# Graph attention on one Trainium2 core: the rows' product with the edge lengths, on VectorE for the next group or on ScalarE for the group two ahead

## What is computed

```python
edge_features = concatenate([h[dst], h[src] * dir_w, dir_w, lower_adj_feat])
edge_attr = edge_features @ W_ee + b_ee
for i in range(3):                      # 3 heads of 128 features
    q, k, v = (x @ Wq[i] + bq[i]), (x @ Wk[i] + bk[i]), (x @ Wv[i] + bv[i])
    e = edge_attr @ We[i] + be[i]
    alpha = (q[dst] * (k[src] + e)).sum(-1) / sqrt(128)
    w = softmax of alpha over the edges of each dst
    out = segment_sum((v[src] + e) * w, dst).mean over heads + x @ Ws[i] + bs[i]
    x = relu(out + residual)
```

## Time and profile before

| | us |
|---|---|
| median of 3 runs | 4367.55 |
| lowest and highest | 4361.53, 4377.33 |
| the profiled execution | 4329.4 |
| its span | 4327.6 |

### The profile page before, as it was taken

How to read it: one execution, slowest core, us unless ns; L and a number is a source line. 1 busy time by engine, 2 the same in 40 slices (tenths; PEclk the granted TensorE clock), 3 DMA queues, 4 the chain that set the end, 5 groups by cost and what they waited for, 6 DMA issues and landing times. The chain is left out here.

```text
span 4327.6 us, 82914 instructions
## 1 busy us (share of the span) xinstructions
PE 3495.6 (81%) x22381; PEld 2067.5 (48%) x22381; DVE 1823.4 (42%) x5369; ACT 1433.0 (33%) x3483; POOL 1862.8 (43%) x1907
## 2 busy tenths in 40 slices
PE   4999999947758888876777777667777769999998
PEld 2666666635534444443444444334443444555564
DVE  4666666647523333332333333323333323344222
ACT  3555555522623333332233323222222223122112
POOL 2555555500256665653566656456666630000000
PEclk8999999979879999998888998878898889999999
DMA  5677775656444554555666666556666645443223
GB/s 139 187 200 199 198 196 167 165 115 204 140 136 137 140 136 131 139 137 136 169 176 172 176 175 179 156 155 167 167 164 168 166 111 176 171 177 118 74 97 125
DMA packets 716528, 675.29 MB, mean 156 GB/s; under 512 B 382359, under 2 KB 542945, under 8 KB 716117
## 3 DMA queue, kind: packets, MB, share of 16 engines
q1 hardware_dynamic: 622598, 466.26, 37.1%
q0 software_dynamic: 77008, 200.24, 17.2%
q10 hardware_dynamic: 16768, 6.91, 0.6%
HBM read 530.84 MB, written 142.28 MB: 156 GB/s over the span
## 5 line engine op out<-in xcount | busy, mean ns | idle before, releaser
L2293 POOL DMA_INDIRECT l_y<-s_lrows,l_src x1344 | 1352.6, 1006 | 964.3 <-issue 352.4
L2373 PE MATMUL ps<-l_y,aw_pT 128*63 128x277 f32 x2700 | 436.8, 467 | 259.9 <-ACT aw_pT L2591 249.1
L3404 PE MATMUL ps<-nl_adj,nl_table 126*128 126x504 bf16 (+1 forms) x3150 | 631.4, 357 | 2.3 <-DVE nl_table L3639 2.3
L998 POOL DMA_INDIRECT em_gs<-s_rows,em_idx x400 | 432.3, 1081 | 325.8 <-DVE em_a L1189 147.9
L2357 PE MATMUL ps<-aw_yT,aw_qt 128*63 128x384 f32 x1800 | 377.2, 529 | 120.0 <-DMA aw_yT<-s_dxT 61.2
L3404 PEld LDWEIGHTS ps<-nl_adj,nl_table 126*128 126x128 bf16 x3150 | 301.8, 96 | 299.0 <-issue 5.3
L2750 DVE COPY aw_axd<-ps 128x252 f32<-128x252 f32 x225 | 94.7, 421 | 796.9 <-remote 409.9
L2330 PE MATMUL ps<-ident,l_y 128*128 128x128 f32 x1800 | 281.5, 292 | 150.9 <-issue 83.1
L2373 PEld LDWEIGHTS ps<-l_y,aw_pT 128*63 128x63 f32 x2700 | 195.7, 154 | 431.9 <-ACT aw_pT L2591 279.6
L2591 ACT ACTIVATE aw_pT<-ps 128x381 f32<-128x381 f32 x225 | 109.9, 488 | 736.8 <-remote 506.0
L2577 ACT ACTIVATE aw_yT<-ps 128x512 f32<-128x512 f32 (+1 forms) x525 | 261.4, 536 | 245.2 <-remote 114.7
(11 more groups left out here) (381 smaller groups left out, 5866.1 us busy)
## 6 DMA issues: line engine op xcount, KB each, us to landing
nl_adj<-s_adj SPq DMA_DIRECT2D x20, 3100.8 KB
aw_yT<-s_dxT SPq DMA_DIRECT2D x150, 384.0 KB
aw_geoS<-s_geoS SPq DMA_DIRECT2D x450, 94.5 KB
nl_adj<-s_adj SPq DMA_DIRECT2D x15, 2325.6 KB
ws_msg<-s_msg SPq DMA_DIRECT2D x75, 384.0 KB, 3.8
s_dxT<-aw_yT SPq DMA_DIRECT2D x75, 384.0 KB
aw_qt<-s_qt SPq DMA_DIRECT2D x225, 126.0 KB
s_msg<-em_msg SPq DMA_DIRECT2D x100, 256.0 KB
```

What stands on the lines that cost most here:

```text
L998: pool.indirect_dma_start(out=gs[:, u, j, :], out_offset=None, in_=d["rows0"], in_offset=bass.IndirectOffsetOnAxis(ap=slot[:, u, 2 * j:2 * ...
L2293: pool.indirect_dma_start(out=y[:, u, j, 0:W], out_offset=None, in_=table, in_offset=bass.IndirectOffsetOnAxis(ap=src[:, u, j:j + 1], axis ...
L2373: m = nc.tensor.matmul(k.ps[64 * v:64 * v + HW, SUM, 0:SW], pT[:, SLOT[u], j, 64 * v:64 * v + HW], y[:, u, v * TH + j, 0:SW], start=j == 0 ...
L3404: m = nc.tensor.matmul(k.ps[:, bank(i, p), 0:cols * WN], source[:, p, q, b, :], adj[:, a % 2, 0:cols, b * WN:(b + 1) * WN], start=b == 0 a ...
```

## The change

The multiplication leaves VectorE. ScalarE does it as six activations of 128 x 128 (Copy with the edge length as a per-partition scale), for the group two ahead instead of the next one: three after the exponentials, three after the copy of the sums. ScalarE waits for the rows, the lengths and the buffer ahead of the first three. The product has a semaphore of its own (`weighed`); TensorE waits for it before the transposes of piece 1 in layer 0, and before the weighted sums in layers 1 and 2. The first two groups of a layer are multiplied before the loop. VectorE's wait for the buffer moves to `mask`. To free semaphores, `query_mixed` and `query_mixed_c` are merged into `mixed` and `mixed_c` (same order, shifted counts); these lines are left out below.

```diff
-    ready = steps("ready", ["DX", "SEL", "OFF"], U, NW)
+    ready = steps("ready", ["SEL", "OFF"], U, NW)
+    weighed = steps("weighed", ["DX"], U, NW)
...
                 if l == 0 and n == 1:
-                    pe.wait_ge(ready.sem, ready.of(w, "DX"))
+                    pe.wait_ge(weighed.sem, weighed.of(w, "DX"))
...
         def sums(w, u):
             pe.wait_ge(pT_ok.sem, pT_ok.of(w, "P"))
             pe.wait_ge(agr_ok.sem, agr_ok.of(w - 1, "AG"))
+            if l:
+                pe.wait_ge(weighed.sem, weighed.of(w, "DX"))
...
+        def weigh(w, u, i, js):
+            if 0 in js:
+                act.wait_ge(rows_in[u], (i + 1) * 16 * T + rows_base[u])
+                act.sem_inc(hop["act"], 1)
+                act.wait_ge(in_[u], (i + 1) * 96 + in_base)
+                act.sem_inc(hop["act"], 1)
+                if started(w, U):
+                    act.wait_ge(summed.sem, summed.of(w - U, "AG"))
+                    act.sem_inc(hop["act"], 1)
+            for j in js:
+                m = nc.scalar.activation(y[:, u, j, D:2 * D], y[:, u, j, W - D:W], ACT.Copy, scale=y[:, u, j, G0:G0 + 1])
+            if T - 1 in js:
+                m.then_inc(weighed.sem, 1)
...
                 copy_features(w + 1, (u + 1) % U, 1, i if u < U - 1 else i + 1)
             exponentials(w, u)
+            ahead = not (isinstance(w, int) and w + 2 >= NW)
+            if ahead:
+                weigh(w + 2, (u + 2) % U, i if u < U - 2 else i + 1, range(0, T // 2))
...
             if started(w, 1):
                 copy_sums(w - 1, (u - 1) % U)
+            if ahead:
+                weigh(w + 2, (u + 2) % U, i if u < U - 2 else i + 1, range(T // 2, T))
             if not last and l == 0:
                 copy_features(w + 1, (u + 1) % U, 2, i if u < U - 1 else i + 1)
...
-        for s in (yT_ok, pT_ok, exped, agr_ok) + ((query_ok,) if queries else ()):
+        for s in (weighed, yT_ok, pT_ok, exped, agr_ok) + ((query_ok,) if queries else ()):
             s.prime(act)
         if before is None:
-            for n in TURNS:
+            copy_features(0, 0, 0, 0)
+            weigh(0, 0, 0, range(T))
+            for n in TURNS[1:]:
...
                 copy_features(0, 0, n, 0)
+            weigh(0, 0, 0, range(T))
         for to, from_ in weights2:
             act.dma_start(to, from_).then_inc(w2_in, 16)
+        weigh(1, 1, 0, range(T))
...
-        def weigh(w, u, i):
-            dve.wait_ge(rows_in[u], (i + 1) * 16 * T + rows_base[u])
-            dve.wait_ge(in_[u], (i + 1) * 96 + in_base)
+        def mask(w, u):
+            s = ready.sem
             if started(w, U):
                 dve.wait_ge(summed.sem, summed.of(w - U, "AG"))
-            nc.vector.tensor_tensor(y[:, u, :, D:2 * D], y[:, u, :, W - D:W], bc(y[:, u, :, G0:G0 + 1], [128, T, D]),
-                                    ALU.mult).then_inc(ready.sem, 1)
-
-        def mask(w, u):
-            s = ready.sem
...
             if not (isinstance(w, int) and w == NW - 1):
-                weigh(w + 1, (u + 1) % U, i if u < U - 1 else i + 1)
                 mask(w + 1, (u + 1) % U)
```

More of the change, by code:

```diff
@@ L2140, in attention_windows @@
         xs = sb("xs", [D, CW])
-        w2_in, query_mixed, query_mixed_c = sem("w2_in"), sem("query_mixed"), sem("query_mixed_c")
+        w2_in = sem("w2_in")
         rows_out, qt_out, qs_out, next_src = sem("rows_out"), sem("qt_out"), sem("qs_out"), sem("next_src")
@@ L2467, in mix_queries @@
                                          start=True, stop=True)
-                m.then_inc(query_mixed, 1)
+                m.then_inc(mixed, 1)
             elif n == 1:
-                pe.wait_ge(query_mixed_c, 2)
+                pe.wait_ge(mixed_c, steps + 2)
                 for h in range(2):
                     m = nc.tensor.matmul(k.ps[:, 6 + h, 0:2 * D + GK], wqT[:, h * D:(h + 1) * D], kb[:, h, :], start=True, stop=True)
-                m.then_inc(query_mixed, 1)
+                m.then_inc(mixed, 1)
             else:
-                pe.wait_ge(query_mixed_c, 4)
+                pe.wait_ge(mixed_c, steps + 4)
                 nc.tensor.matmul(k.ps[:, 6, 0:2 * D + GK], wqT[:, 2 * D:3 * D], kb[:, 2, :], start=True, stop=True)
@@ L2513, in turn @@
                 if queries:
-                    pe.wait_ge(query_mixed_c, 7)
+                    pe.wait_ge(mixed_c, steps + 7)
                 pe.wait_ge(mixed_c, steps)
@@ L2770, in mix_queries @@
         def mix_queries(n):
-            dve.wait_ge(query_mixed, n + 1)
+            dve.wait_ge(mixed, n + 2)
             if n == 0:
-                nc.vector.tensor_copy(wqT[:, :], k.ps[:, 6, 0:H * D]).then_inc(query_mixed_c, 1)
+                nc.vector.tensor_copy(wqT[:, :], k.ps[:, 6, 0:H * D]).then_inc(mixed_c, 1)
                 nc.vector.tensor_copy(kb[:, :, D:2 * D + GK], k.ps[:, 7, 0:H * (D + GK)].rearrange("p (h f) -> p h f", h=H)
-                                      ).then_inc(query_mixed_c, 1)
+                                      ).then_inc(mixed_c, 1)
             elif n == 1:
                 for h in range(2):
-                    nc.vector.tensor_copy(abc[:, h, :], k.ps[:, 6 + h, 0:2 * D + GK]).then_inc(query_mixed_c, 1)
+                    nc.vector.tensor_copy(abc[:, h, :], k.ps[:, 6 + h, 0:2 * D + GK]).then_inc(mixed_c, 1)
             else:
-                nc.vector.tensor_copy(abc[:, 2, :], k.ps[:, 6, 0:2 * D + GK]).then_inc(query_mixed_c, 1)
+                nc.vector.tensor_copy(abc[:, 2, :], k.ps[:, 6, 0:2 * D + GK]).then_inc(mixed_c, 1)
                 bias_of = k.ps[:, 7, 0:3 * H].rearrange("p (h t) -> p h t", t=3)
-                nc.vector.tensor_copy(ab[:, :, 0:2], bias_of[:, :, 0:2]).then_inc(query_mixed_c, 1)
-                nc.vector.tensor_copy(ab[0:GK, :, 2:3], bias_of[0:GK, :, 2:3]).then_inc(query_mixed_c, 1)
+                nc.vector.tensor_copy(ab[:, :, 0:2], bias_of[:, :, 0:2]).then_inc(mixed_c, 1)
+                nc.vector.tensor_copy(ab[0:GK, :, 2:3], bias_of[0:GK, :, 2:3]).then_inc(mixed_c, 1)
         def split_geometry(c):
@@ L2839, in vector @@
             dve.sem_inc(indexed.sem, U)
-        weigh(0, 0, 0)
         mask(0, 0)
```

## The result

The changed kernel took 4423.5 us (median of 4 runs) against 4364.5 us for the kernel before on the same chip: 1.0137 of it, 95% interval 1.0101 to 1.0172. It is slower by 59 us; 26 us less was forecast, and the time lies above the range's upper end. The profiled execution took 4428.4 us, its span 4426.6.

A forecast was written before the change was run, and what follows sets the result against it. TensorE, busy 81% of the span, was taken as nearest to a bound, its waits differing by layer. -30 (a) -31 (b) +32 (c) +3 (d) = -26 us, from 4367.55 to 4341.5 us; 8-in-10 range 4285 to 4403 us.

The forecast's parts named there:

- (a): Layer 0: TensorE's wait for VectorE's multiplication goes; 30 us gained, bounds 0 and 43.
- (b): GpSimd's gathers, no longer held up by VectorE's multiplication, free 75 us of GpSimd; 31 us gained, bounds 0 and 75.
- The fifth that I gave layer 1: Layer 1's share of the gathers' saving: 5 us gained, a fifth, since SyncE's load issues bound that layer.
- (c): Layer 0: ScalarE's copies delay the third feature copy, 34 groups at 0.93 us; 32 us lost, bounds 14 and 70.
- (d): Layers 1 and 2: ScalarE's added copies mostly fit its idle time before the next weights' copy; 3 us lost.
- the cover of 4.3 us: Layers 1 and 2: ScalarE's idle time ahead of the next weights' copy, set against 1.9 us of added copies a group.
- its own sample: Layer 0 trace sample: both halves of the copies stand between exponential and third feature copy, 1.9 us more on the path.
- Moved waits: ScalarE now waits for gather and loads of the group two ahead; nothing taken, bounds 0 to 25 us lost.
- rival 4: Layer 1: ScalarE stands for SyncE's loads, key copies come late, TensorE waits; +25 us there; chance 0.25 together with rival 2.
- Rival 3: Layer 0: nearly every group waits for the third feature copy, 70 us lost; +40 in all, 4407 us; chance 0.21.
- Layer 1 within 10 us: Sign in the profile after: layer 1's length changes by at most 10 us; over 20 us would refute the prediction.

The follow-up runs named there:

- the first of the experiments: First comparison, on a chip with late releases: e1, e2, e3n and e3w, each against the kernel before; ratios 1.0043, 1.0081, 1.0081 and 1.0104.
- e3n: Kernel before plus six ScalarE copies into an unread tile at the changed kernel's places, without its waits for rows and loads: 1.0081 of the kernel before.
- e2: Changed kernel plus VectorE's old two-operand operation at its old place, into a tile nobody reads: 4402.2 us, 1.0081 of the kernel before.
- e3w: Kernel before plus six ScalarE copies into an unread tile, with the changed kernel's waits for rows, loads and buffer: 1.0104 of the kernel before.
- e1: VectorE keeps its one multiplication but for the group two ahead, with the changed kernel's semaphores and no ScalarE copies: 4379.5 us, 1.0043 of the kernel before.

## Why the prediction was wrong, point by point

With late releases, as in the profile that I read, the ratios split the 59 us: removal alone +25 us (0.0058), the copies at the end of the turn +4 (0.0010, not told from nothing), their place in the middle +30 (0.0069). These come from two comparisons; the first of the experiments gives nearly the same by another way. There the copies in the middle, with the product still on VectorE, cost 0.0081 (e3n); with the removal's 0.0058 that makes 0.0139, where the change cost 0.0137. And putting VectorE's old operation back took off 0.0056 (e2).

- **(a) TensorE's wait for the product, -30 us.** It went, as forecast: no row of L2331 for it in layer 0, but for the 5.2 us at its start. What I named as late next took it: the third feature copy with 55.1 us. With quick releases the wait was 20.8 us and went too.
- **(b) The gathers, -31 us.** This is the step that failed. That they fall to 0.95 us was right to 2 ns (948), and that 75 us of GpSimd are freed too (77.9). That freed time of GpSimd is worth something where "releases wait on the gathers' burst" had the wrong sign. (a) and (b) together are the removal: forecast -61, measured -68 to -81 us with quick releases (0.9818 to 0.9785) and +25 with late ones. Wherever (a) lay within its bounds, 0 to 43 us gained, a sum of +25 leaves a loss for (b). The rows of late releases were in my hand, and I took them for a gain. They said that the loop's length is set by when events arrive, and no row said that shorter gathers make these arrive sooner. The right reading was to leave (b) open on both sides; "bounds 0 and 75" excluded a loss without a reason. The fifth that I gave layer 1, "since SyncE bounds it", was no better founded: with quick releases the removal took 35 us off just that layer (589.2 to 553.9).
- **(c), (d) ScalarE's order, +32 and +3 us.** The copies have the forecast length: three in 1.00 us (3203.17) where I took 0.93. The sum, 35, is near as well, +34 us with late (30 for the place, 4 for the copies) and +43 with quick releases. By layer, layer 0 has most of it, 21 of 32 us with quick releases and 34 of 57 in e3n with late ones; what layers 1 and 2 pay with late ones, and so whether the cover of 4.3 us held, these traces don't tell. One thing in (c) didn't fit: its own sample had both halves on the path, 1.9 us, and the sum took 0.93 us for each group.
- **Moved waits, 0 of 0 to 25 us.** ScalarE stood for the loads, 35.6 us in layer 1 and 46.1 us in layer 2, as rival 4 had it. What the wait costs wasn't told from nothing (e3w against e3n, +10 us), and the 19 us of e1 hold the same wait on VectorE together with the operation's leaving its old place, which alone costs 25.
- **Rivals.** Rival 3 gave 4407 us and the right direction by half the cause; it priced the gathers at -10. None had the mechanism that decided, a removal that costs. With quick releases the sum of the forecast, -26 us, meets what was measured, -30 us, partly by luck: the removal and the order of the copies were both some 8 us larger, and that cancels.
- **What would show it.** "Layer 1 within 10 us" failed, it is 36 us longer, and I had written that 20 would refute the forecast. The gathers' mean, the copies' length and, nearly, TensorE's wait in layer 0 (55 us of some 65) came out as written, which says how little they vouch for the sum.

Open: why releases come late in some comparisons only, and by which way the removal lengthens the loop there: through VectorE's place, the gathers' bursts or the granted clock. Whether a one-operand operation on VectorE would do e2's good wasn't seen with late releases.

## What to carry to other kernels

Where a profile shows engines idle behind events that come microseconds after the instruction, time freed on an engine need not be time freed on the path, and here it cost 25 us: price such a removal from both sides of nothing. When work moves to an engine that relays a loop (here ScalarE between two steps of TensorE), put it at the end of that engine's turn: the same six copies cost 30 to 43 us in the middle here and nothing that could be told at the end. And run a change of under 2% on more than one chip before it is kept: this one is 1.4% slower on one kind and 0.8% faster on the other.

## What the runs showed of the hardware

- The same program takes 4320 to 4366 us in three comparisons, at a granted clock of 0.913 to 0.924, and 3759 to 3771 us in four, on four other chips, at 0.942 to 0.951. The difference lies where gathers run: what follows the last exponential, without a gather, is 792 us on one kind and 788 us on the other, and layer 1 is 731 and 589 us. An event of TensorE inside a stretch of gathers comes 1.8 to 2.5 us late in the mean on the one, at most 0.11 us on the other (at most 0.24 us in the changed kernel), and SyncE's instructions of over 0.55 us, register loads left out, sum in layer 1 to 2.6 us a group on the one and 0.95 us on the other.
- VectorE's two-operand form holds up gathers, 1004 to 1013 ns in the mean against 948 to 954 without it; six one-operand operations leave 960 ns, a one-operand reduction of 935 ns beside ScalarE's copies 954 ns, and ScalarE's copies alone 948 to 954 ns, as does no product at all (951 to 954).
- A Copy on ScalarE of 128 elements with its scale read from a tile takes 389 to 398 ns in the mean, and three in a row 0.97 to 1.00 us.
